# Limits of the second attention chosen on GpSimd, evacuations moved ahead of a wait, reciprocals of the last mixture taken once per batch

## The reference, cut to what matters

```
h = token_map(x)                                   # (2, 1024, 1024)
h = h + attention0(layernorm(h))                   # 32 heads, 8 key heads, causal softmax
h = h + mixture0(layernorm(h))                     # top-2 of 8 low-rank experts plus a base matrix
h = h + attention1(layernorm(h))                   # the "second attention"
h = h + mixture1(layernorm(h))                     # all 8 low-rank experts, softmax weights

# attention1, per head (32 heads of 32 columns, 8 key heads), 1024 rows:
draft = q @ k.T, future keys masked
keep  = the 128 largest entries of each row of draft
out   = softmax(draft / sqrt(32), kept and not future) @ v
return out.reshape(...) @ Wo.T
```

## Time and profile before

| What | us |
|---|---|
| profiled execution, its own time | 5241.05 |
| its span, first to last instruction | 5239.3 |
| what lies around the span | 1.75 |
| busy in it: TensorE / VectorE / ScalarE / GpSimd | 4055.4 / 3461.8 / 2811.4 / 41.8 |
| second attention, first limits to last output copy | 2190.2 to 4779.4 |
| last mixture, first load to the end | 4787.5 to 5239.3 |

### The profile page before, as it was taken

The page is one execution under the profiler, slowest core; times in us unless marked ns, Lnnn a source line. Parts: engine busy times, 40 slices in busy tenths (PEclk is TensorE's granted clock), DMA queues, the critical chain, the costliest instruction groups (busy, mean ns, idle before and its releaser), DMA issues. The chain is left out here.

```text
span 5239.3 us, 83348 instructions
## 1 busy us (share of the span) xinstructions
PE 4055.4 (77%) x25610; PEld 2321.0 (44%) x25752; DVE 3461.8 (66%) x10257; ACT 2811.4 (54%) x6546; POOL 41.8 (1%) x85
## 2 busy tenths in 40 slices
PE   6998999998999999546674667667667767758766
PEld 3445766665444444223442334334334434434333
DVE  3556777774333355488778888877878887874555
ACT  1115777774000011378875788788888788871000
POOL 1000000000000000000000000000000000000000
PEclk8999999999999999767876777777778777868888
DMA  4236232232111132301110111100111110103232
GB/s 144 67 75 172 53 78 65 65 85 79 48 48 48 45 73 68 64 21 26 27 23 4 27 27 23 26 14 18 26 27 26 23 26 5 26 6 93 72 73 65
DMA packets 307653, 259.69 MB, mean 50 GB/s; under 512 B 188416, under 2 KB 241936, under 8 KB 307152
## 3 DMA queue, kind: packets, MB, share of 16 engines
q1 hardware_dynamic: 306608, 253.79, 19.0%
q0 software_dynamic: 544, 0.07, 0.0%
HBM read 175.95 MB, written 77.86 MB: 48 GB/s over the span
## 5 line engine op out<-in xcount | busy, mean ns | idle before, releaser
L1063 ACT ACTIVATE a_sign<-arena,a_state 128x384 fp8e4<-128x384 f32 (+5 forms) x1056 | 917.7, 871 | 102.1 <-DVE a_state L1199 61.2
L959 PE MATMUL a_ps_s<-k,q 128*128 128x512 bf16 (+3 forms) x1474 | 463.3, 452 | 608.6 <-DVE arena L1297 404.5
L1030 ACT ACTIVATE a_probT<-a_ps_t 128x512 f32<-128x512 f32 (+3 forms) x768 | 365.7, 483 | 341.8 <-PE a_ps_t L978 262.1
L959 PEld LDWEIGHTS a_ps_s<-k,q 128*128 128x128 bf16 x1536 | 158.7, 124 | 818.9 <-DVE arena L1297 456.3
L971 PE MATMUL a_ps_t<-ident,arena 128*128 128x128 f32 x1584 | 336.1, 329 | 217.4 <-ACT a_probT L1030 182.9
L1063 ACT ACTIVATE a_sign<-a_third,a_state 128x384 fp8e4<-128x384 f32 (+2 forms) x480 | 417.3, 871 | 77.9 <-DVE a_state L1199 75.1
L737 ACT ACTIVATE a_prob<-a_x_neg,a_shift 128x640 f32<-128x640 f32 (+7 forms) x512 | 397.2, 776 | 89.2 <-DVE a_x_neg L780 63.6
L780 DVE TENSOR_SCALAR_CACHE_REDUCE a_x_neg<-a_ps_s 128x640 f32<-128x640 f32 (+7 forms) x512 | 378.8, 752 | 41.7 <-PE a_ps_s L661 26.5
L1210 DVE MAX8 a_nine<-a_below 128x8 f32<-128x256 f32 (+6 forms) x448 | 371.0, 828 | 35.2 <-issue 2.6
L676 PE MATMUL a_ps_t<-ident,a_prob 128*128 128x128 f32 x2304 | 365.6, 282 | 35.1 <-issue 12.0
L997 PE MATMUL a_ps_o<-a_probT,vals 128*64 128x128 f32 x4608 | 364.9, 300 | 0.0
(11 more groups left out here) (254 smaller groups left out, 6685.3 us busy)
## 6 DMA issues: line engine op xcount, KB each, us to landing
q<-qk SPq DMA_DIRECT2D x256, 256.0 KB, 4.5
qk<-p_qkT SPq DMA_DIRECT2D x32, 960.0 KB, 6.2
h_rows<-h SPq DMA_DIRECT2D x32, 512.0 KB, 6.8
k<-qk SPq DMA_DIRECT2D x256, 64.0 KB, 4.9
h<-tok_h SPq DMA_DIRECT2D x16, 512.0 KB, 4.0
arena<-in_wo SPq DMA_DIRECT2D x16, 512.0 KB, 10.7
o<-a_o SPq DMA_DIRECT2D x16, 512.0 KB, 2.7
q<-o SPq DMA_DIRECT2D x16, 512.0 KB, 5.6
```

The lines of the kernel that those rows point to most:

```text
L959: nc.tensor.matmul(ps_s[:, n % 2, a:a + w], q[:, y, head, i * P:(i + 1) * P], k[:, y, a:a + w], start=(y == 0), stop=False, skip_group_che ...
L1030: nc.scalar.activation(probT[:, n % 4, 0:w], ps_t[:, (n + 1) % 2, 0:w], ACT.Exp).then_inc(probT_ready, 1)
L1063: ins = nc.scalar.activation(to, xs[mine][:, at:at + w], ACT.Sign, scale=-1.0, saturate=False, bias=state[:, par, 0, n:n + 1], accum_out=s ...
```

## The change

In the second attention `choose` and the split of the row maxima (`split_top`) go to GpSimd, which has neither the fused scalar-tensor-tensor form, the reductions nor the predicated copy in this code, so that `choose` is built from 27 smaller instructions. VectorE raises `ranked` after the ranks of pass 1; in pass 2 it fetches its four score tiles first and waits for `chosen` before `any_failing` and the masks, and it waits for `top_ready` of the pair before before it fetches. ScalarE issues the evacuations of a pass's first step before it waits for the limits, and the rule weighs the 40 of `BETWEEN` at the start of a pass in place of its end: chunks 0 to 5 now come in step 0, 6 in step 1, 7 in 4, 8 in 5, 9 in 9, 10 and 11 in 11, 12 in 12, 13 in 13 (the end of pass 0); in pass 1, chunks 14 to 16 in its first step, 17 to 22 within it and 23 at its end.

The totals of a batch (32 heads x 1024 rows) are loaded once as a compact tile of 128x256, inverted by one reciprocal, stored to a DRAM tensor `inv1` and loaded spread over the partitions, as the totals were. The reciprocal for batch 0 comes after slot 32, that for batch 1 after the first residual of the last mixture. The load of tile j+4's o and inverses now waits for `added` of tile j (its projection has been read), the store of a tile and the load of h come two steps later in SyncE's loop.

```diff
-def load_totals(sp, j, to, total_dram, arrived):
+def load_inverse(sp, j, to, inv_dram, arrived):
...
-def scale(nc, dve, o, total):
-
-    nc.vector.reciprocal(total, total)
-    dve.drain()
-    return nc.vector.tensor_tensor(o, o, total, ALU.mult)
+def compact_rows(sp, b, rows, dram, moved, load):
+
+    w = T // 4
+    for f in range(4):
+        at, there = rows[f * H:(f + 1) * H, :], dram[:, b * T + f * w:b * T + (f + 1) * w]
+        sp.dma_start(at if load else there, there if load else at).then_inc(moved, 16)
...
                         if not more and y == 0:
-                            load_totals(sp, 0, first_total, total_dram, first_in)
+                            compact_rows(sp, 0, compact, total_dram, inverted, True)
                             meanwhile(sp)
+                            sp.wait_ge(inverted, LOADED + 1)
+                            compact_rows(sp, 0, compact, inv_dram, inverted, False)
+                            sp.wait_ge(inverted, LOADED + 1 + 16 * 4)
+                            load_inverse(sp, 0, first_inv, inv_dram, first_in)
...
-                    counted = [sum(2 + i for _, i in (RANKED * EVAC_PASSES)[:k] if i > 1) + BETWEEN * (k // NS)
+                    counted = [sum(2 + i for _, i in (RANKED * EVAC_PASSES)[:k] if i > 1) + BETWEEN * ((k + NS - 1) // NS)
...
                     def count(p):
 
+                        evacs(p * NS)
                         if p == 0:
                             act.drain()
                         wait_alone(act, t_ready, s * PASSES + (p + 1), const_in, 48)
...
                                 if n:
                                     act.drain()
-                                evacs(p * NS + n)
+                                    evacs(p * NS + n)
...
+                    def choose():
+
+                        off_aim = state[:, y, 1, :]
+                        wait_alone(pool, ranked, s, const_in, 48)
+                        nc.gpsimd.tensor_scalar(state[:, y, 3, SHORT[0]:SHORT[1] + 1:SHORT[1] - SHORT[0]],
...
+                        nc.gpsimd.tensor_scalar(equal[:, :], over[:, :], 2.0 / WIDE, 0.0, ALU.mult, ALU.add)
+                        nc.gpsimd.tensor_copy(nine[:, :, 0], state[:, y, 0, :])
+                        pool.drain()
+                        nc.gpsimd.tensor_tensor(off_aim, state[:, y, 3, :], aim, ALU.subtract)
+                        pool.drain()
...
+                        for w in (4, 2, 1):
+                            nc.gpsimd.tensor_tensor(pick[:, :, :, 0:w], pick[:, :, :, 0:w], pick[:, :, :, w:2 * w], ALU.add)
+                            pool.drain()
...
+                        nc.gpsimd.tensor_tensor(code[:, 0:1], marked[:, 0:1], marked[:, 1:2], ALU.add).then_inc(chosen, 1)
+
+                    def split_top():
+
+                        hi, mid, lo = (top_parts[:, (turn_of + 1) % 3, c * 2 * TT:(c + 1) * 2 * TT] for c in range(SPLITS))
+                        wait_alone(pool, x_ready, (s + 2) * (2 * TT), const_in, 48)
+                        nc.gpsimd.tensor_scalar(neg[:, :], top[:, :], -1.0, 0.0, ALU.mult, ALU.add)
+                        pool.drain()
+                        nc.gpsimd.tensor_copy(top_b[:, 0, :], neg[:, :])
...
+                        nc.gpsimd.tensor_tensor(lo, rest[:, :], top_b[:, 1, :], ALU.subtract).then_inc(top_ready, 1)
+
+                    if st["keep"]:
+                        choose()
+                    if st["score"]:
+                        split_top()
...
                             if p == 1:
-                                choose()
-                            if p == 2:
-                                any_failing()
+                                dve.sem_inc(ranked, 1)
                         if p == 2 and st["value"]:
                             dve.wait_ge(turn_done, (s - 2) * TURNED + TURNED)
...
                         if p == 2:
+                            if st["score"] and not (isinstance(s, int) and s < 0):
+                                dve.wait_ge(top_ready, s + 1)
+                            for n in fetches:
+                                fetch(n)
+                            if keeps:
+                                dve.wait_ge(chosen, s)
+                                any_failing()
                             for r in keeps:
                                 mark(r).then_inc(mask_ready, 1)
                             if keeps:
                                 exact_where_needed()
                             dve.drain()
-                            for n in fetches:
-                                fetch(n)
...
+                    if isinstance(s, int) and s == PAIRS:
+                        dve.wait_ge(inverted, LOADED)
+                        nc.vector.reciprocal(compact[:, :], compact[:, :]).then_inc(inverted, 1)
...
-                for j in range(NT):
-                    sp.wait_ge(y_ready, j + 1)
-                    sp.dma_start(out_dram[j * P:(j + 1) * P, :], y[:, j % 2, :]).then_inc(y_out[j % 2], 16)
+                for j in range(NT + 2):
+                    if j + RING == TT:
+                        sp.wait_ge(inverted, LOADED + 1 + 16 * 4)
                     if j + RING < NT:
+                        sp.wait_ge(added, 2 * j + 2)
                         load_o(j + RING)
-                        load_h(j + RING)
+                    if j == 0:
+                        sp.wait_ge(inverted, LOADED + 1)
+                        compact_rows(sp, 1, compact, inv_dram, inverted, False)
+                    if j >= 2:
+                        sp.wait_ge(y_ready, j - 1)
+                        sp.dma_start(out_dram[(j - 2) * P:(j - 1) * P, :], y[:, j % 2, :]).then_inc(y_out[j % 2], 16)
+                        if j - 2 + RING < NT:
+                            load_h(j - 2 + RING)
...
-                    scale(nc, dve, o[:, j % RING, :], totals[:, j % RING, :]).then_inc(scaled, 1)
+                    nc.vector.tensor_tensor(o[:, j % RING, :], o[:, j % RING, :], inverse[:, j % RING, :],
+                                            ALU.mult).then_inc(scaled, 1)
...
                 residual(0)
+                dve.wait_ge(inverted, LOADED)
+                nc.vector.reciprocal(compact[:, :], compact[:, :]).then_inc(inverted, 1)
```

## The result

The kernel after takes **5208.97 us** in the median of five runs (5195.72 to 5213.65), the kernel before 5235.53; the ratio is 0.9942, with a 95% interval of 0.9926 to 0.9958. The change wins 0.6%, which is 26.6 us between the medians, where 64 were forecast. The profiled execution took 5201.94 us, its span 5200.1, against 5239.3 before.

| Stretch | before | after | difference | forecast |
|---|---|---|---|---|
| up to the first limits of the second attention | 2190.2 | 2189.6 | -0.6 | 0 |
| its first limits to its last output copy | 2588.0 | 2687.0 | +99.0 | +71 |
| last output copy to the mixture's first load | 9.3 | 4.3 | -5.0 | -4.1 |
| mixture's first load to the end | 451.8 | 319.2 | -132.6 | -131 |

What follows compares the result with a forecast made beforehand. Bounds: a ScalarE-VectorE ring in the second attention, and a chain through VectorE and loads in the last mixture. Mixture -135 plus attention +71 gives -64: 5177 profiled, 5172 median; own range 5145 to 5195, 8-in-10 range 5065 to 5240.

Steps and rivals of the forecast that it cites:

- The mixture: Last mixture: projections 18.36 us apart at TensorE's pace, first load some 4.1 us earlier; -135 us.
- Rival D: Last mixture: loads and stores in small pieces hold a tile at 24 us, 73 us lost, 5245; chance 0.10.
- The attention: Second attention: +2.5 us per pair over 30 pairs, with -6 and +1.6 elsewhere; +71 us in all.
- the clock over all pairs: Pass 1 of the second attention: -1.8 us, taken as -1.3 over all pairs because TensorE's clock sometimes rises earlier.
- The first two pairs: First two pairs of the second attention, where VectorE is late: 6 us saved in all.
- cover: Pass 2 of the second attention: 10.6 us of GpSimd's chain, taken as 9 us, stay hidden from VectorE.
- Rival B: Pass 2: GpSimd's chain takes 15.9 us, VectorE waits 5.3 us past its cover per pair, 5331; chance 0.10.
- Rival C: VectorE's narrowing beside GpSimd: waits at the shared SBUF port cost 1.5 us a pair, +45, 5217; chance 0.12.
- Rival A: Second attention: TensorE at full clock from the six early turns, a pair at -1.55 us, 5050; chance 0.20.

Runs made afterwards that it cites:

- mix_only: Kernel after with the rule, the place of the evacuations, and the choice and split put back as before, leaving only the mixture's part; 5105.38 us.
- rule_no_lead: Kernel after with the first evacuations of a pass back behind the wait for its limits, the new spreading rule kept; 5237.67 us.
- mix_gpsimd_lead: Kernel after with only the spreading rule put back to that of the kernel before; 5056.53 us.
- mix_rule_lead: Kernel after with the choice of limits and the split back on VectorE; 5192.74 us.
- gpsimd_long: Kernel after with one product pair of GpSimd's choice done six times in place of once; 5299.76 us.
- mix_gpsimd: Kernel after with the rule and the place of the evacuations put back as before, GpSimd's and the mixture's parts kept; 5086.74 us.
- keep_busy: Kernel after with eight unread TensorE matmuls, six ahead of the twelfth turn and two ahead of the thirteenth; 5169.16 us.
- the control: Kernel after with eight unread matmuls, six and two ahead of the fifth and sixth turn, where TensorE is busy anyway; 5177.65 us.
- after_warm44: Kernel after with unread matmuls in TensorE's idle time, 44 ahead of the third turn and 3 ahead of the fourth; 5128.87 us.

## Why the prediction was right and wrong

**Right in its steps, off in two terms.** The forecast was 5172; 5209 was measured, inside the range of 5065 to 5240 and outside the forecast's own range of 5145 to 5195.

*The mixture.* 18.36 us a period forecast from the one pair of tiles that had run without waiting; 18.29 measured, 13 times. Tile 2's projection starts 43.6 us after the first load, against 45.7 before, and the first load goes 4.3 us after the last output copy where it was 9.3. -135 forecast, -138 in the trace, -131 in mix_only's medians. Rival D (24 us a tile) did not happen: the DMA engines were busy 38% in the steady stretch.

*The attention, sum by sum.* In the pair shown the forecast holds: the pair was to be 80 us against 77.6 and is 79.26, the six evacuations end 5.6 us after the limits, where 6 was said, and VectorE's wait before the first narrowing is 7.60, where 7 or more was said. Over the 28 pairs the parts of a pair took, in the mean (us; a pass is counted to the start of its narrowing, "other" are the 23 that aren't long):

| Part | before | after | difference | forecast | 5 long | 23 other |
|---|---|---|---|---|---|---|
| limits to the end of pass 0 | 15.81 | 22.06 | +6.25 | | 22.46 | 21.98 |
| pass 1 | 18.92 | 18.12 | -0.80 | -1.3 | 20.65 | 17.57 |
| pass 2 | 14.54 | 13.10 | -1.44 | -1.65 | 13.06 | 13.11 |
| pass 3 | 12.94 | 12.92 | -0.02 | 0 | 13.01 | 12.91 |
| last narrowing to the next limits | 15.08 | 14.34 | -0.74 | | 14.46 | 14.31 |

The first and the last line belong together, since the limits now come earlier and ScalarE's evacuations don't: +5.51, where +5.5 was forecast. The lead gained 1.4 us a pair in rule_no_lead and the rule's price follows from mix_gpsimd_lead.

*The term that failed: the clock over all pairs.* The step was "where the clock rises earlier, TensorE is quicker and there is less to win; I take -1.3 over all pairs". It measured -0.80: -1.35 in the 23 other pairs, +1.73 in the five long ones, which as whole pairs are 3.8 us longer than the others. The step looked only at the time of the rise, and took it that the clock then stays. In seven of the 30 pairs it fell back, which the new places bring about themselves: evacuations wait behind longer stretches of counting, TensorE idles there, and the clock falls just ahead of the turns of pass 1 that need TensorE most. It takes the rule and the lead together. Half clock for 6.8 us or more after the rise, beginning in the first 34 us of a pair, is found in 7, 5 and 7 of 30 pairs of after, mix_rule_lead and gpsimd_long, and in none of before, mix_only, mix_gpsimd, mix_gpsimd_lead and rule_no_lead.

The attention's miss of 28 us (99 against 71) is made up of the 28 pairs at +3.26 against +2.5, 21 us; the exact-search pair at +6.5 against +2.5, 4 us; and the first two pairs at -3.0 against -6, 3 us. By the table the 21 are 14 in pass 1, 6 in pass 2 and 1 of rounding. keep_busy took 16 us off pass 1 of the 28 pairs and 3 off that of the exact-search pair (17.64 us against 20.68) with only TensorE's idle time filled, and the control kept falls; so for the failed term the falls are shown as the cause. The 6 us of pass 2 are the size of what the slower narrowing beside GpSimd costs in mix_rule_lead's comparison. The Trainium skill, TensorE: Matmul & The Clock Gate, section A second HAM failure mode: psum-queue depth-cycling, tells of a kernel whose clock swings because TensorE idles for short times between groups of matmuls; the rows of the long pair (1.08 and 0.21 us of waiting, then half clock) agree with it. The median missed by 37 us, the profiled executions by 25 (5201.9 against 5177): before's stood 5.5 us above its median, after's 7.0 below.

*The first two pairs.* -6 taken, -3.0 measured (61.8 and 69.2 us against 62.8 and 71.2). That was a guess without rows, and half of it was wrong.

*GpSimd.* 9 us forecast, 9.6 to 10.2 measured; cover 10.6 forecast, 11.3 by gpsimd_long. Rival B was a real cliff, and the change stands 1.5 us from it.

*Rival C, the port.* It was right in kind and too high in price. The 11 instructions of the narrowing beside GpSimd's chain take 0.20 us more together, where the rival had 1.5 us a pair (11 x 0.125 is 1.4). By the rule that the prediction cited from the Trainium skill, SBUF — State Buffer, section Who interferes with whom, VectorE and GpSimd should exclude each other here for a whole instruction at a time; the trace agrees in that instructions grow longer (L1258's by 43 ns, L1254's by 40, L1253's by 14 in the mean of pass 1), and the sum is about a seventh of what I had made of it. mix_gpsimd gained where this rival had it lose.

*Rival A, the turns go fast.* It needed the full clock from the early turns on and gave a pair of 77.28 - 1.55 = 75.7 us. The kernel after has no such pair. after_warm44 made some: with the clock full from 1.6 us before the limits the pair took 75.7. The arithmetic held; the condition did not.

**What the change did in all:** -130.6 us from the mixture, -18.6 from GpSimd's part and -30.2 from the lead at the old places, +152.4 from the rule; together -27.0, where the medians of the two kernels differ by 26.6. The order matters: taken out of the kernel after, GpSimd's part wins nothing.

## What to carry to other kernels

Where a schedule is worked out from weights, a change in the rule moves every instruction: compute the new order, and price each pass, not the edit's intent. An engine whose clock follows its own load has to be checked for the idle gaps that a new order makes, since pauses of some 1.3 us ahead of its busiest stretch were followed by a loss of four in seven pairs of 30 here; a few unread matmuls there are a cheap test. Take a bundled change apart early: one of these four parts cost what two others won, and without it the kernel is 2.9% faster.

## What the runs showed that was not expected

- Pauses of 1.08 and 0.21 us were followed by 10.2 us at half clock, and 0.5 us of unread work put into them kept it at full. In an ordinary pair of the same kernel (limits at 3744.47) TensorE was no busier at that point, 1.86 of 3.40 us, and the clock held, so I draw no threshold from it.
- Sixteen back-to-back 128x128 bf16 matmuls took 1.43 us, and 44 took 2.63 us at the full clock; the same kind amid other work counts 225 to 308 ns each in the groups. An idle stretch needs far more of them than the group's mean says.
- VectorE's instructions of 0.17 to 0.22 us grew by up to 43 ns in the mean while GpSimd worked through short ones, and the whole narrowing by a tenth.
- A GpSimd instruction of 128x14 took 0.21 to 0.38 us in the mean of its group, one of 128x112 0.38 to 0.61 us, and a drained step left 0.15 us between.
